# Expert layer of a two-layer network: the experts' sum is copied out of PSUM by ScalarE, and two VectorE passages are cut in two

## The reference

```
# x: 8 batches x 512 tokens x 256 features, float32
y   = moe(x, cond)                       # 8 experts, two per token, and a shared part
x   = x + ternary_linear(y)              # y quantised to 8 bits per token
x   = x + ffn(attention(x, bias, mask))  # 16 heads with causal bias, then an 8-bit FFN
```

## Time and profile before

| | |
|---|---|
| Median of three runs | 1453.21 us |
| Lowest, highest | 1450.84, 1454.32 us |
| Profiled execution, its own time | 1449.1 us |
| Span of its trace | 1447.0 us |
| Mean granted TensorE clock | 0.949 of full speed |
| Busy over the span | TensorE 1255.0 us (87%), VectorE 1035.3 (72%), ScalarE 763.9 (53%), GpSimd 553.6 (38%) |

### The profile page before, as it was taken

The page is one execution under the profiler, slowest core; times in us unless marked ns, Lnnn a source line. Parts: engine busy times, 40 slices in busy tenths (PEclk is TensorE's granted clock), DMA queues, the critical chain, the costliest instruction groups (busy, mean ns, idle before and its releaser), DMA issues. The chain is left out here.

```text
span 1447.0 us, 29659 instructions
## 1 busy us (share of the span) xinstructions
PE 1255.0 (87%) x8705; PEld 998.7 (69%) x8710; DVE 1035.3 (72%) x2788; ACT 763.9 (53%) x1940; POOL 553.6 (38%) x834
## 2 busy tenths in 40 slices
PE   4999989998973699999999999999999999944866
PEld 2777877787861478778777877877787788831223
DVE  5566666656555677887887888878878878763986
ACT  3223223232221466676766767666677677624853
POOL 1333323232322576445344444454454545510014
PEclk9999999999985799999999999999999999976987
DMA  6233212210204400001000010010010000202115
GB/s 231 63 128 103 74 51 80 102 72 15 88 15 135 163 15 2 2 2 31 2 19 16 2 31 2 1 32 2 2 31 2 6 12 1 76 14 64 58 56 176
DMA packets 51039, 71.52 MB, mean 49 GB/s; under 512 B 4497, under 2 KB 43665, under 8 KB 48850
## 3 DMA queue, kind: packets, MB, share of 16 engines
q1 hardware_dynamic: 50338, 69.60, 14.4%
q10 hardware_dynamic: 560, 0.20, 0.1%
HBM read 57.07 MB, written 12.72 MB: 48 GB/s over the span
## 5 line engine op out<-in xcount | busy, mean ns | idle before, releaser
L844 POOL TENSOR_SCALAR scores<-scores,att_rinv 128x128 f32<-128x128 f32 (+3 forms) x512 | 264.2, 532 | 195.9 <-DVE att_rinv L1056 195.9
L900 ACT ACTIVATE scores<-scores,att_top 128x128 f32<-128x128 f32 (+3 forms) x512 | 281.6, 553 | 78.5 <-DVE att_top L1038 78.1
L1038 DVE CUSTOM_DVE_ANT_0 scores<-ps_y,w_bias_b,null_s 128x128 f32<-128x128 f32 x448 | 229.6, 547 | 85.3 <-PE ps_y L1188 78.9
L261 POOL TENSOR_TENSOR act_w<-act_g,wide_w 128x512 f32<-128x512 f32 x64 | 105.6, 1649 | 279.7 <-DVE act_g L379 274.1
L1187 PE MATMUL ps_y<-k_hh,q_hl 128*128 128x256 f32 (+2 forms) x512 | 190.6, 381 | 14.8 <-DVE att_top L1038 7.4
L908 ACT ACTIVATE keep<-ps_up 128x128 f32<-128x128 f32 (+3 forms) x256 | 111.9, 437 | 167.7 <-PE ps_up L1199 163.8
L1199 PE MATMUL ps_up<-ident,scores 128*128 128x128 f32 x1280 | 190.6, 274 | 9.9 <-DVE keep L1066 9.2
L208 ACT ACTIVATE hid_hi<-hid 128x512 fp32r<-128x512 f32 x80 | 50.5, 631 | 241.8 <-DVE hid L397 241.7
L1199 PEld LDWEIGHTS ps_up<-ident,scores 128*128 128x128 f32 x1280 | 150.7, 140 | 31.1 <-issue 13.0
L1210 PE MATMUL ps_a<-keep,w_val 128*64 128x128 f32 x2560 | 171.0, 281 | 0.7 <-DVE keep L1066 0.7
L851 POOL TENSOR_SCALAR w_q_hm<-q_hl 64x512 fp32r<-64x512 f32 x128 | 76.6, 611 | 227.9 <-ACT q_hl L923 227.9
(11 more groups left out here) (236 smaller groups left out, 2585.0 us busy)
## 6 DMA issues: line engine op xcount, KB each, us to landing
wide_w<-token_w_dram SPq DMA_DIRECT2D x16, 1024.0 KB, 4.6
x_raw<-in_x_t_dram SPq DMA_DIRECT2D x8, 512.0 KB, 3.8
x_nat<-in_x_nat_dram SPq DMA_DIRECT2D x8, 512.0 KB, 4.8
x_dram<-x_nat SPq DMA_DIRECT2D x8, 512.0 KB, 2.9
w_x1t<-x_dram SPq DMA_DIRECT2D x8, 512.0 KB, 4.3
c_dram<-out_raw SPq DMA_DIRECT2D x8, 512.0 KB, 3.2
c2t<-c_dram SPq DMA_DIRECT2D x8, 512.0 KB, 3.7
x_tile<-x_dram SPq DMA_DIRECT2D x8, 512.0 KB, 4.3
```

What stands on the lines that cost most here:

```text
L261: nc.gpsimd.tensor_tensor(act_w[:, k % 2], act_g[:, k % 2], wide_w[:, k], ALU.mult).then_inc(sem.act_w_ready, 1)
L844: nc.gpsimd.tensor_scalar(s, s, rinv[:, pp, q, hh:hh + 1], 0.0, ALU.mult, ALU.add).then_inc(sem.p_normed, 1)
L900: nc.scalar.activation(s, s, ACT.Exp, scale=-1.0, bias=top[:, pp, q, hh:hh + 1], accum_out=lsum[:, pp, q, hh:hh + 1]).then_inc(sem.exp_don ...
L1038: dve.tensor_tensor_reduce(scores_of(pp, hh, q), psS[:, hh, 0:n], bias_of(w, h)[:, CAUSAL[q]:CAUSAL[q] + n], 1.0, null_s[:, par, q, h:h + ...
```

## The change

Three things change, all in the queues of ScalarE and VectorE in `moe_phase`.
- ScalarE copies ps_y to SBUF (`y_sb`, a view of `gate_raw`) in one instruction, between `leak_part` and `hidden_hi` of step 1. It waits for the last `down` of the last batch and signals `y_read`, for which TensorE now waits.
- `quantise` is cut in two and reads `y_sb`: `quantise_scales` behind `hidden` of step 1, `quantise` (four scalings and the widening) behind `hidden` of step 2.
- `route` is cut in two: `route_scores` (up to the two comparisons) behind `hidden` of step 3, the rest behind `hidden` of step 4.

No instruction of VectorE is added or removed; ScalarE has one more per batch. TensorE's, GpSimd's and SyncE's queues stay as they are.

```diff
--- before.py
+++ after.py
@@ -104,6 +104,7 @@
         yq_t = sb("yq_t", [P, HC, S], BF16)
 
         y = ps.y[:].rearrange("p a (t n) -> p (a t) n", n=H)
+        y_sb = gate_raw[:, 0, 0:TT * H].rearrange("p (t n) -> p t n", n=H)
         z_bf = ps.a1[:].bitcast(BF16).rearrange("p (c s) -> p c s", c=HC)
         z_out = ps.a1[:].rearrange("p (t n) -> p t n", n=H)
 
@@ -191,6 +192,12 @@
                     act.wait_ge(sem.wt_done, f + 1)
                     nc.scalar.activation(weight_t[:], ps.a2[0:E, :], ACT.Copy).then_inc(sem.wt_ready, 1)
 
+                def experts_out(b):
+                    act.wait_ge(sem.d_done, NE * (b + 1))
+                    if not known(b, 1):
+                        act.wait_ge(sem.yq_ready, b)
+                    nc.scalar.activation(y_sb, y, ACT.Copy).then_inc(sem.y_read, 1)
+
                 def quantised_out(b):
                     act.wait_ge(sem.yqt_done, b + 1)
                     nc.scalar.activation(yq_t[:], z_bf, ACT.Copy).then_inc(sem.yqt_ready, 1)
@@ -213,6 +220,8 @@
                         if ahead and k == 0:
                             split_hi(b + 1, 1 - par)
                         leak_part(s, k % 2)
+                        if behind and k == 1:
+                            experts_out(b - 1)
                         if ahead and k == 2:
                             logits_out(b + 1)
                         if ahead and k == 3:
@@ -248,6 +257,7 @@
                     batch(2 * j + 1, 1, True, True)
                     batch(2 * j + 2, 0, True, True)
                 batch(B - 1, 1, True, False)
+                experts_out(B - 1)
                 quantised_out(B - 1)
 
             @block.gpsimd
@@ -310,7 +320,7 @@
                     nc.vector.tensor_tensor(shift[:], logits, top[:].unsqueeze(2).broadcast_to([P, TT, E]),
                                             ALU.subtract).then_inc(sem.shift_ready, 1)
 
-                def route(f):
+                def route_scores(f):
 
                     dve.wait_ge(sem.ex_ready, f + 1)
                     wide = lambda t: t[:].unsqueeze(2).broadcast_to([P, TT, E])
@@ -325,6 +335,9 @@
                     nc.vector.tensor_tensor(ge[:], other, own, ALU.is_ge)
                     nc.vector.tensor_tensor(gt[:], other, own, ALU.is_gt)
                     dve.drain()
+
+                def route():
+                    wide = lambda t: t[:].unsqueeze(2).broadcast_to([P, TT, E])
                     nc.vector.tensor_tensor(ge[:], ge[:], gt[:], ALU.subtract)
                     dve.drain()
                     nc.vector.tensor_tensor(ge[:], ge[:], w.earlier[:].unsqueeze(1).broadcast_to([P, TT, E, E]), ALU.mult)
@@ -344,10 +357,10 @@
                     dve.drain()
                     nc.vector.tensor_tensor(token_w[:], rank[:], wide(top), ALU.mult).then_inc(sem.w_ready, 1)
 
-                def quantise(b, par):
-
-                    dve.wait_ge(sem.d_done, NE * (b + 1))
-                    nc.vector.tensor_reduce(amax[:], y, X, ALU.max, apply_absolute_value=True)
+                def quantise_scales(b, par):
+
+                    dve.wait_ge(sem.y_read, b + 1)
+                    nc.vector.tensor_reduce(amax[:], y_sb, X, ALU.max, apply_absolute_value=True)
                     dve.drain()
                     nc.vector.tensor_scalar(amax[:], amax[:], 1e-5, None, ALU.max)
                     dve.drain()
@@ -356,9 +369,10 @@
                     dve.drain()
                     nc.vector.tensor_scalar(qscale[:], qscale[:], Q, None, ALU.mult)
                     dve.drain()
+
+                def quantise(b):
                     for t in range(TT):
-                        last = nc.vector.tensor_scalar(y8[:, t], y[:, t], qscale[:, t:t + 1], None, ALU.mult)
-                    last.then_inc(sem.y_read, 1)
+                        nc.vector.tensor_scalar(y8[:, t], y_sb[:, t], qscale[:, t:t + 1], None, ALU.mult)
                     dve.drain()
                     nc.vector.tensor_copy(yq[:], y8[:]).then_inc(sem.yq_ready, 1)
 
@@ -403,15 +417,19 @@
                         leaky(s, k % 2)
                         if not (first and k == 0):
                             hidden_lo(s - 1, 1 - k % 2)
-                        if behind and k == 1:
-                            quantise(b - 1, 1 - par)
                         if ahead and k == 0:
                             split_lo(b + 1, 1 - par)
                         if ahead and k == 3:
                             softmax_shift(b + 1)
                         hidden(b, k)
+                        if behind and k == 1:
+                            quantise_scales(b - 1, 1 - par)
+                        if behind and k == 2:
+                            quantise(b - 1)
+                        if ahead and k == 3:
+                            route_scores(b + 1)
                         if ahead and k == 4:
-                            route(b + 1)
+                            route()
                         if behind and k == 6:
                             residual(b - 1, 1 - par, 0)
                         if behind and k == 8:
@@ -426,7 +444,8 @@
                 weight_lo(ROUTER)
                 softmax_shift(0)
                 dve.wait_ge(sem.ident, 6)
-                route(0)
+                route_scores(0)
+                route()
                 weight_lo(GATE)
                 weight_lo(UP)
                 weight_lo(DOWN)
@@ -443,7 +462,8 @@
                     batch(2 * j + 2, 0, False, True, True)
                 batch(B - 1, 1, False, True, False)
                 hidden_lo(NE * B - 1, 1)
-                quantise(B - 1, 1)
+                quantise_scales(B - 1, 1)
+                quantise(B - 1)
                 residual(B - 1, 1, 0)
                 residual(B - 1, 1, 1)
```

## The result

The changed kernel took 1432.76 us (median of 4 runs, 1432.26 to 1433.24) against 1453.03 us for the kernel before in the same comparison: a ratio of 0.9859, interval 0.9845 to 0.9873. The forecast was 1432.5 us. The profiled execution took 1432.46 us, its span is 1430.5 us, the mean granted clock 0.949.

A forecast was written before the change was run, and what follows sets the result against it. A repeating ScalarE, VectorE and GpSimd chain, 4.35 us a turn, bounds the kernel. Savings 12.8 + 9.0 - 1.6 + 1.0 - 0.5 = 20.7 us give 1428.4 profiled, 1432.5 against the median; range 1427 to 1441.

The forecast's parts named there:

- The ring: Expert loop: leak, act_g, act_w, hid, hid_hi follow each other, 4.35 us a turn, without TensorE, and set the batch time.
- TensorE's wait: Rival: TensorE standing 18.7 us for ps_y before down is a bound of its own, giving 1426; chance 0.05.
- The terms: VectorE pieces behind hid, per batch over the free gaps: quantisation 1.41 instead of 3.24 us, routing 2.40 instead of 3.68.
- Batch 1: GpSimd, busy with attention bias, delays hid of step 1; quantisation saves 0.2 us instead of 1.8, so 1.6 less.
- The clock: TensorE's granted clock no longer falls to 0.50 behind the ps_y wait: 1.0 us saved over the phase.
- The tail: Last quantisation has nothing to hide behind; copy adds 1.02 + 0.06, SBUF reads take off 0.55: 0.5 us more.
- The copy at nothing: ScalarE's 1.02 us copy behind leak of step 1 costs nothing; margin 2.6 us for down(b-1, 9) ending late.
- TensorE behind it: TensorE, freed from the ps_y wait, runs ahead until down(4), idle 1 to 2 us there for hid_lo.
- Contention: Rival: GpSimd slows scalings and cast, 0.72 us each in 7 batches, 10.1 us lost, giving 1442.6; chance 0.14.
- the 4.1 added for the median: The profiled execution lay 4.1 us below the median of three runs, so 1428.4 became 1432.5.

The follow-up runs named there:

- routing alone: The kernel before with only the routing cut in two behind hid of steps 3 and 4: 1443.49 us, ratio 0.9952.
- the copy alone: The kernel before plus the ScalarE copy of ps_y, quantisation whole in its old place but reading SBUF, routing whole: 1452.77 us, ratio 1.0004.
- the doubled copy: The changed kernel with the ScalarE copy of ps_y made twice, once into an unused buffer: 1432.61 us, ratio 0.9871.
- the experiment: The changed kernel with scalings and cast ahead of hid of step 2, while GpSimd runs act_w, instead of behind it: 1439.58 us, ratio 0.9925.
- the kernel in smaller pieces: The changed kernel with VectorE's side work in ten pieces around hid in steps 0 to 5, weights one step later: 1418.32 us, ratio 0.9774.

## Why the prediction was right, and where it was not

- **What bounds the loop.** The ring, not TensorE's wait: routing alone gained 0.48% with that wait untouched, the copy alone took it away and gained nothing.
- **The terms.** This is where the sum was short. The forecast had 46.75 us for a batch (49.86 less 3.11), measured were 47.07. The turns of steps 1 to 5 were to be 4.4, 5.2, 4.9, 4.7 and 6.4, and came as 4.35, 5.39, 4.88, 4.84 and 6.40. The sizes of the reduce (1.19 forecast, 1.21), scalings (1.11, 1.13) and cast (0.69) held. Two turns are longer than their terms (4.35 + 0.88 and 4.35 + 0.33) by 0.16 each, and nearly all of that is one thing: each time `act_g` follows the last small instruction of a piece later than priced (183.01 to 183.40 is 0.39 against the 0.25 usual, 192.49 to 193.13 is 0.64 against 0.50). I had left out what a piece's end costs. 0.28 us a batch is 2 us in seven.
- **Batch 1.** As forecast, `hid` of step 1 waited for GpSimd and came 5.53 us behind its `leak` (80.29 and 85.82), and that turn took 6.79 us. The batch went from 50.91 us (`leak` at 75.67 and 126.58) to 49.84 (74.88 and 124.72): 1.07 saved where 1.5 was forecast (0.2 + 1.28).
- **The clock.** Up to the last `down` the kernel before had five stretches at the lower level, in batches 0, 1, 2, 4 and 5; the changed kernel has one, in batch 1 behind a wait of 1.93 us at 90.16, where the forecast had none. Before, batches 2, 4 and 5 took 50.40, 50.00 and 50.16 us against 49.85 of batch 3, 1.0 us more in all. Batches 2 to 6 saved 3.11, 2.78, 2.96, 3.09 and 2.84 us; what goes beyond the 2.78 of batch 3, which had the full clock in both, is 0.9 in all. So the term of 1.0 held, though no run changed the clock alone.
- **The tail.** From the first reader of the last `down` to the barrier 15.04 us (404.75 to 419.79) instead of 14.52: 0.52 more, forecast 0.5.
- **The copy at nothing.** Shown by the doubled copy. In batch 7 it waited 1.53 us for `down(9)` (at 365.78), and its turn was 4.41 us like its neighbours.
- **TensorE behind it.** Forecast 1 to 2 us idle at `down(4)`: 1.54.
- **The rivals.** Contention would have cost 1.05 us for the scalings (2.18 less 1.13) had they been placed beside GpSimd; in the change's places it cost nothing. The 0.72 that the rival counted for the scalings was too small. The 7.0 us that the experiment lost (1439.58 against 1432.61 of the doubled copy beside it) are 1.0 a batch, but also hold the gap behind `hid` that it leaves empty.
- **The number.** The expert phase gained 18.0 us where 20.7 was forecast. Batch 0 gave 0.8 instead of 1.28, batch 1 1.07 instead of 1.5, batches 2 to 6 2.78 each instead of 3.11. The term that the sum had at nothing, the pieces' ends, makes 2.0 of the difference, spread over these batches; the other 0.6, of which 0.35 in batch 0, stays open. The span fell by 16.5, as the phases behind took 1.5 us more; why, no run tells apart from scatter. The profiled execution of before lay 3.9 us under its median, that of after 0.3 under. So 1432.5 met the median more closely than its terms deserved: against 1428.4 the profiled execution came 4.1 us higher, and the 4.1 added for the median were not there again. That the two errors cancel is luck. In the comparisons of the experiments the kernel before had medians of 1450.3 to 1451.0 us; against those 1432.76 is a gain of about 18, as the phase's own 18.0.

## What to carry to other kernels

When an engine that looks bound waits, follow the chain of instructions that repeats each turn and see whether the engine is in it; a wait of an engine outside it moves when it is removed, and the time stays, unless the engine comes so late that a member of the ring waits for it. Inside such a ring, measure the gap that each member leaves, cut the side work to pieces that fit behind the instruction that ends the gap, and count what ends a piece too, here about 0.15 us for each piece that stands before the next member. A copy that only frees a buffer may bring nothing alone and still be what makes the better order possible.

## What the runs showed of the hardware

VectorE instructions beside GpSimd's `act_w`, from the kernel in smaller pieces:

```profile
175.31 1.67 POOL L271 TENSOR_TENSOR act_w<-act_g,wide_w 128x512 f32<-128x512 f32 x1 [2.68 <-DVE act_g L401]
...
175.93 1.08 DVE L371 TENSOR_SCALAR amax<-amax 128x4 f32<-128x4 f32 x1
...
185.50 1.66 POOL L271 TENSOR_TENSOR act_w<-act_g,wide_w 128x512 f32<-128x512 f32 x1 [3.56 <-DVE act_g L401]
...
185.94 1.50 DVE L337 TENSOR_TENSOR gt<-score 128x256 f32<-128x256 f32 x1
```

A tensor_scalar of 128x4 took 1.08 us instead of 0.17, ending at 177.01 as `act_w` ended at 176.98; the comparison `gt` of 128x256 took 1.50 instead of 0.42, ending 0.28 us behind `act_w`. `x_lo` took 2.31 us beside it before (from 178.88, with `act_w` ending at 180.12) and 1.21 behind `hid`. The price is thus not a share of the instruction: it is 0.91, 1.08 and 1.10 us where GpSimd still had 1.05, 1.22 and 1.24 to go, whatever the size. The four scalings of the run beside GpSimd paid 1.05 with 1.23 to go. The reduce met no such price: in the run of the copy alone it took 1.21 us from SBUF at 235.22, beside an `act_w` from 234.79 to 236.46, as it did with GpSimd idle. The Trainium skill (SBUF — State Buffer, Who interferes with whom) says that the engine that comes second fully blocks, that `tensor_scalar` can take both ports, that two SBUF inputs contend with GpSimd's reads, and that `tensor_reduce` never contends on this chip. The durations agree, but for 0.14 to 0.18 us by which each price is below the whole rest of `act_w`.

The clock after a wait wasn't the same each time. Before, behind the waits of 2.94 us that ended at 137.75, 238.01 and 288.00 the granted clock was 0.50 for about 3.5 us (the earlier trace rows has the first), but it stayed at 1.00 behind one of 2.94 us that ended at 338.18 and one of 2.90 at 188.15. What parts them these runs don't tell.
